# A four-block fp32 kernel on one Trainium2 core: cached keys taken transposed from a DRAM scratch, and the output projection of attention dealt out anew

## What is computed

```python
q = rope(rmsnorm(x @ Wq.T, q_norm_w)); k = rope(rmsnorm(x @ Wk.T, k_norm_w)); v = x @ Wv.T
kc = k_cache[block_table].reshape(bsz, 512, 8, 128)      # 16 pages of 32 keys per batch row
vc = v_cache[block_table].reshape(bsz, 512, 8, 128)
k_all, v_all = concat([kc, k], 1), concat([vc, v], 1)    # 640 keys
scores = einsum('bqhd,bkhd->bhqk', q, repeat(k_all, 4)) / sqrt(128)
scores = where(valid, scores, -1e30)                     # cached keys at or past cache_seqlens are masked
o = einsum('bhqk,bkhd->bqhd', softmax(scores), repeat(v_all, 4))
x = x + o.reshape(bsz, seqlen, 4096) @ Wo.T
```

## Time and profile before

| | |
|---|---|
| median of 3 runs | 1541.6 us |
| profiled execution | 1539.51 us, its span 1537.7 us |
| busy: PE, DVE, ACT, POOL | 96%, 73%, 55%, 49% of the span |
| mean granted TensorE clock | 0.987 |
| matmuls of PE | 8254 instructions |
| HBM read, written | 97.9 MB, 2.1 MB |

### The profile page before, as it was taken

The page is one execution under the profiler, slowest core; times in us unless marked ns, Lnnn a source line. Parts: engine busy times, 40 slices in busy tenths (PEclk is TensorE's granted clock), DMA queues, the critical chain, the costliest instruction groups (busy, mean ns, idle before and its releaser), DMA issues.

```text
span 1537.7 us, 27396 instructions
## 1 busy us (share of the span) xinstructions
PE 1468.6 (96%) x8254; PEld 1267.7 (82%) x8254; DVE 1117.8 (73%) x2224; ACT 851.5 (55%) x2024; POOL 750.0 (49%) x700
## 2 busy tenths in 40 slices
PE   3899999999999999999999999999997998999999
PEld 2788888888888888888888888888886776888887
DVE  4788888888888888888888888888885554122212
ACT  1566666666666666666666666666653233332331
POOL 5555565555655566555565555654440002433442
PEclk9899999999999999999999999999998999999999
DMA  4422222222222222222222222213202301331331
GB/s 123 136 62 77 59 59 65 63 67 72 59 64 65 62 75 60 63 65 71 67 59 64 64 65 74 59 46 110 52 15 59 87 0 39 108 102 51 104 102 63
DMA packets 107461, 105.99 MB, mean 69 GB/s; under 512 B 35873, under 2 KB 79393, under 8 KB 107073
## 3 DMA queue, kind: packets, MB, share of 16 engines
q1 hardware_dynamic: 107328, 104.42, 23.9%
HBM read 97.91 MB, written 2.10 MB: 65 GB/s over the span
## 4 chain that ended last, share of the span: by engine, by line
PE 72%; DVE 18%; issue 7%; ACT 1%; DMA 1%; POOL 1%; DVEq 0%; SPq 0%; ACTq 0%; POOLq 0%
PE banks L279 21%; PE banks L281 21%; PE banks L280 21%; PE banks L1106 8%; DVE pt_pair L739 3%; DVE k_sin L727 3%; DVE q_cos L720 3%; DVE kv_raw L733 2%; DVE w_pair L785 2%; DVE o_pair L739 1%; DVE k_cos L727 1%; DMA w_raw<-in_w_att 1%; PE banks L1171 1%; POOL w_pair L430 1%; DVE kv_raw L734 0%
## 5 line engine op out<-in xcount | busy, mean ns | idle before, releaser
L580 ACT ACTIVATE prob<-prob,nbias 128x640 f32<-128x640 f32 x256 | 210.2, 822 | 168.7 <-DVE nbias L763 168.7
L763 DVE CUSTOM_DVE_ANT_0 prob<-banks,mask,q_rs 128x640 f32<-128x640 f32 x256 | 219.5, 874 | 66.5 <-PE banks L281 66.4
L739 DVE TENSOR_TENSOR pt_pair<-banks,pt_pair 128x640 fp32r<-128x640 f32 x256 | 209.4, 818 | 61.2 <-ACT pt_pair L576 61.1
L576 ACT ACTIVATE pt_pair<-banks 128x640 fp32r<-128x640 f32 x256 | 179.2, 700 | 62.0 <-PE banks L1106 62.0
L1106 PE MATMUL banks<-ident,prob 128*128 128x128 f32 x1280 | 184.2, 275 | 19.1 <-DVE pt_pair L739 19.1
L773 DVE TENSOR_SCALAR prob<-prob,rsum 128x640 f32<-128x640 f32 x256 | 193.1, 754 | 9.1
L279 PE MATMUL banks<-w_pair,x_pair 128*128 128x256 f32 (+1 forms) x512 | 179.2, 350 | 21.1 <-POOL w_pair L430 21.1
L1106 PEld LDWEIGHTS banks<-ident,prob 128*128 128x128 f32 x1280 | 150.6, 141 | 49.7 <-issue 31.8
L509 POOL TENSOR_TENSOR fw_pair<-w_raw,fw_pair 128x1280 fp32r<-128x1280 f32 (+1 forms) x44 | 98.5, 2260 | 162.2 <-ACT fw_pair L672 154.6
L280 PE MATMUL banks<-w_pair,x_pair 128*128 128x256 f32 (+1 forms) x512 | 173.8, 339 | 0.0
L281 PE MATMUL banks<-w_pair,x_pair 128*128 128x256 f32 (+1 forms) x512 | 173.7, 339 | 0.0
(11 more groups left out here) (198 smaller groups left out, 3708.6 us busy)
## 6 DMA issues: line engine op xcount, KB each, us to landing
kv_raw<-in_kv SPq DMA_DIRECT2D x1024, 32.0 KB, 1.7
w_raw<-in_w_att SPq DMA_DIRECT2D x64, 320.0 KB, 3.0
w_raw<-in_fw SPq DMA_DIRECT2D x66, 256.0 KB, 2.9
x_raw<-in_xT SPq DMA_DIRECT2D x64, 256.0 KB, 3.1
w_raw<-gu_b SPq DMA_DIRECT2D x44, 64.0 KB, 2.9
acc<-in_x SPq DMA_DIRECT2D x1, 2048.0 KB, 10.5
w_raw<-in_w SPq DMA_DIRECT2D x2, 1024.0 KB, 5.3
out_x<-acc SPq DMA_DIRECT2D x8, 256.0 KB, 2.3
```

What stands on the lines that cost most here:

```text
L576: act.activation(pt_pair[:, 0, h].rearrange("p c n -> p (c n)"), pt_ps, ACT.Copy).then_inc(pt_hi, 1)
L580: act.activation(prob[:, h, :], prob[:, h, :], ACT.Exp, bias=nbias[:, h:h + 1], scale=-1.0, accum_out=psum_row[:, h:h + 1]).then_inc(exped, 1)
L739: dve.tensor_tensor(pair[1], src, pair[0].bitcast(F32), ALU.subtract).then_inc(lo_sem, 1)
L763: dve.tensor_tensor_reduce(out=prob[:, h, :].rearrange("p (a n) -> p a n", a=2), in0=score_ps[h % 2][:, :, 0:HALF], in1=mask[:, n % B, :]. ...
```

## The change

The host hands over a second copy of the key cache, `kT`, with each page transposed to heads x (128 x 32). A scratch tensor `kt_all` is made in DRAM, batch row x page slot x head x 128 x 32. In steps 0 to 7 SP, after the loads of the step, reads the page numbers of batch row n again and issues 16 DMAs from `kT` to `kt_all` (`gather_keys`), each 8 rows of 16 KB. From the second group on (steps 8 to 63) the cached keys of a step come with one DMA from `kt_all` to `kt_raw` (128 partitions, each 16 runs of 128 bytes), ahead of the step's page DMAs, which then carry only the values. ACT splits off the high half of `kt_raw` in a copy of its own (128x512) and that of the new keys from PSUM (128x128); POOL makes the cached keys' low half (`kc_low`), DVE that of the new keys alone. PE's cached-key transposes remain for steps 0 to 7 only. PE issues the 12 output matmuls as 2 ahead of the transposes of head 1, 8 after them and 2 after those of head 2. On DVE `w_high` stands ahead of `mask_min` of head 2, and `kt_low` ahead of `pt_low` of head 1. The scratch for dynamic DMA descriptors is 4096 instead of 8192.

```diff
--- before.py
+++ after.py
@@ -106,6 +106,7 @@
         x_pair = [sb(f"x_pair{i}", [P, 2, DC, P], F32R, where=att) for i in range(2)]
         kv_raw = sb("kv_raw", [P, 2, KC, 2 * D], where=att)
         v_pair = [sb(f"v_pair{i}", [P, 2, KC, D], F32R, where=att) for i in range(2)]
+        kt_raw = sb("kt_raw", [P, 2, CACHE], where=att)
         kt_pair = sb("kt_pair", [P, 2, KEYS], F32R, where=att)
         qt_pair = sb("qt_pair", [P, 2, REP, P], F32R, where=att)
         pt_pair = sb("pt_pair", [P, 2, REP, KC, P], F32R, where=att)
@@ -225,6 +226,9 @@
         k_rot = sem("k_rot")
         kt_done = sem("kt_done")
         kt_hi, kt_lo = sem("kt_hi"), sem("kt_lo")
+        s_gathered = [sem(f"s_gathered{b}") for b in range(B)]
+        s_ktin = [sem(f"s_ktin{i}") for i in range(2)]
+        kc_hi, kc_lo = sem("kc_hi"), sem("kc_lo")
         scored = sem("scored")
         masked = sem("masked")
         exped = sem("exped")
@@ -272,6 +276,8 @@
         td_done, td_own, td_hi, td_lo = sem("td_done"), sem("td_own"), sem("td_hi"), sem("td_lo")
         ffn_done, ffn_added = sem("ffn_done"), sem("ffn_added")
 
+        kt_all = nc.dram_tensor("kt_all", [B, NPP, HK, D, PSIZE], F32, kind="Internal").ap()
+
         block = ctx.enter_context(nc.Block())
 
         def product(e, dst, lhs, rhs, first, last):
@@ -302,18 +308,37 @@
             def load_w(m, par):
                 sp.dma_start(w_raw[:, par, :], t["w_att"][ds(m), :, :].rearrange("a p n -> p (a n)")).then_inc(s_win[par], 16)
 
-            def load_kv(n, par, used=False):
-                g, b = n // B, n % B
+            def load_pages(b):
                 _, pages = nc.values_load_multi_w_load_instructions(
                     t["pages"][ds(b), :], engines=[sp.engine], min_val=0, max_val=PAGES - 1,
                     skip_runtime_bounds_check_because="page numbers are below PAGES")
+                return pages
+
+            def load_kv(n, par, used=False):
+
+                g, b = n // B, n % B
+                pages = load_pages(b)
+                if g:
+                    if n >= B + 2:
+                        sp.wait_ge(kc_lo, n - B - 1)
+                    if g == 1:
+                        sp.wait_ge(s_gathered[b], 16 * NPP)
+                    sp.dma_start(kt_raw[:, par, :].rearrange("p (j s) -> p j s", s=PSIZE),
+                                 kt_all[b, :, g].rearrange("j d s -> d j s")).then_inc(s_ktin[par], 16)
                 if used:
                     sp.wait_ge(v_lo, n - 1)
                     sp.wait_ge(kt_done, n - 1)
+                at = D if g else 0
                 for j, page in enumerate(pages):
                     a = PSIZE * (j % 4)
-                    sp.dma_start(kv_raw[a:a + PSIZE, par, j // 4, :],
-                                 t["kv"][ds(g), ds(page), :, :].rearrange("g a s n -> s (g a n)")).then_inc(s_kvin[par], 16)
+                    sp.dma_start(kv_raw[a:a + PSIZE, par, j // 4, at:2 * D],
+                                 t["kv"][ds(g), ds(page), :, at:2 * D].rearrange("g a s n -> s (g a) n")).then_inc(s_kvin[par], 16)
+
+            def gather_keys(b):
+
+                for j, page in enumerate(load_pages(b)):
+                    sp.dma_start(kt_all[b, j].rearrange("g d s -> g (d s)"),
+                                 t["kT"][ds(page), :, :].rearrange("a g n -> (a g) n")).then_inc(s_gathered[b], 16)
 
             load_x(0, 0)
             load_w(0, 0)
@@ -356,6 +381,8 @@
             last_w = NT - PIECES - 1
             for n in range(NT - 2):
                 step(n, n % 2, x=n + 3 < NT, w=n < last_w)
+                if n < B:
+                    gather_keys(n)
                 if n == NT - PIECES + 1:
                     _, labels = nc.values_load_multi_w_load_instructions(
                         t["label"].unsqueeze(0), engines=[sp.engine], min_val=0, max_val=4,
@@ -435,6 +462,11 @@
                 pool.tensor_tensor(v_pair[par][:, 1], kv_raw[:, par, :, D:2 * D],
                                    v_pair[par][:, 0].bitcast(F32), ALU.subtract).then_inc(v_lo, 1)
 
+            def kc_low(n, par):
+                pool.wait_ge(kc_hi, n - B + 1)
+                pool.tensor_tensor(kt_pair[:, 1, 0:CACHE], kt_raw[:, par, :], kt_pair[:, 0, 0:CACHE].bitcast(F32),
+                                   ALU.subtract).then_inc(kc_lo, 1)
+
             def q_norm(n, par):
 
                 pool.wait_ge(q_sq, n + 1)
@@ -482,6 +514,8 @@
                     q_rotate(n + 1)
                     q_norm(n + 1, 1 - par)
                 v_low(n, par)
+                if nxt and n + 1 >= B:
+                    kc_low(n + 1, 1 - par)
                 if isinstance(n, int) and n == 0:
                     w_low(PIECES - 1, 1)
                 if x:
@@ -564,8 +598,12 @@
                 act.activation(qt_pair[:, 0].rearrange("p h n -> p (h n)"), q_ps, ACT.Copy).then_inc(qt_hi, 1)
 
             def kt_high(n):
+                new = slice(CACHE if n >= B else 0, KEYS)
                 act.wait_ge(kt_done, n + 1)
-                act.activation(kt_pair[:, 0], kt_ps, ACT.Copy).then_inc(kt_hi, 1)
+                if n >= B:
+                    act.wait_ge(s_ktin[n % 2], 16 * ((n - B) // 2 + 1))
+                    act.activation(kt_pair[:, 0, 0:CACHE], kt_raw[:, n % 2, :], ACT.Copy).then_inc(kc_hi, 1)
+                act.activation(kt_pair[:, 0, new], kt_ps[:, new], ACT.Copy).then_inc(kt_hi, 1)
 
             def o_high(n):
                 act.wait_ge(pv_done, n + 1)
@@ -742,7 +780,8 @@
                 low(qt_hi, n + 1, [qt_pair[:, k].rearrange("p h n -> p (h n)") for k in range(2)], q_ps, qt_lo)
 
             def kt_low(n):
-                low(kt_hi, n + 1, [kt_pair[:, k] for k in range(2)], kt_ps, kt_lo)
+                new = slice(CACHE if n >= B else 0, KEYS)
+                low(kt_hi, n + 1, [kt_pair[:, k, new] for k in range(2)], kt_ps[:, new], kt_lo)
 
             def o_low(n):
                 low(o_hi, n + 1, [o_pair[:, k].rearrange("p h n -> p (h n)") for k in range(2)], misc_ps, o_lo)
@@ -824,6 +863,10 @@
                 if not first:
                     pt_low(n - 1, 3)
                 normalise(n, 1)
+                if first:
+                    w_high(PIECES - 1, 1)
+                if w:
+                    w_high(n + PIECES, par)
                 mask_min(n, par, 2)
                 if nxt:
                     q_times_cos(n + 1)
@@ -831,19 +874,14 @@
                 normalise(n, 2)
                 if n + 1 < B:
                     make_mask(n + 1)
-                if first:
-                    w_high(PIECES - 1, 1)
-                if w:
-                    w_high(n + PIECES, par)
                 if not first:
                     o_low(n - 1)
                 pt_low(n, 0)
                 mask_min(n, par, 3)
                 if nxt:
                     qt_low(n + 1)
+                    kt_low(n + 1)
                 pt_low(n, 1)
-                if nxt:
-                    kt_low(n + 1)
                 normalise(n, 3)
                 pt_low(n, 2)
                 if not first:
@@ -1083,12 +1121,16 @@
 
             def transpose_new_k(n, par):
                 pe.wait_ge(k_rot, n + 1)
+                if n >= B:
+                    pe.wait_ge(masked, REP * (n - 1) + 3)
                 pe.transpose(kt_ps[:, CACHE:KEYS], kv_raw[:, par, KC - 1, 0:D], ident[:]).then_inc(kt_done, 1)
 
             def scores(n, h):
                 if h == 0:
                     pe.wait_ge(qt_lo, n + 1)
                     pe.wait_ge(kt_lo, n + 1)
+                    if n >= B:
+                        pe.wait_ge(kc_lo, n - B + 1)
                 elif h > 1:
                     pe.wait_ge(masked, REP * n + h - 1)
                 elif not (isinstance(n, int) and n == 0):
@@ -1118,15 +1160,17 @@
                                    c == 0, c == KC - 1)
                 last.then_inc(pv_done, 1)
 
-            def project_out(n, heads):
-                if heads[0] == 0:
+            def project_out(n, begin, end):
+
+                if begin == 0:
                     pe.wait_ge(o_lo, n + 1)
                     pe.wait_ge(w_lo, (n // B) * PIECES + PIECES)
                 at = group_at(n) + WWO
-                for h in heads:
-                    last = product(pe, misc_ps, lambda k: o_pair[:, k, h, :],
-                                   lambda k: w_pair[:, k, ds(at + h * HID, HID)], h == 0, h == REP - 1)
-                if heads[-1] == REP - 1:
+                for i in range(begin, end):
+                    h, (j, k) = i // 3, ((0, 0), (0, 1), (1, 0))[i % 3]
+                    last = pe.matmul(misc_ps, o_pair[:, j, h, :], w_pair[:, k, ds(at + h * HID, HID)],
+                                     start=i == 0, stop=i == 3 * REP - 1)
+                if end == 3 * REP:
                     last.then_inc(wo_done, 1)
 
             def step(n, par, x=True, w=True, nxt=True):
@@ -1145,14 +1189,17 @@
                 scores(n, 3)
                 if nxt:
                     transpose_q(n + 1)
```

(14 more changed lines are left out.)

## The result

The changed kernel takes 1572.9 us (median of 4 runs), the kernel before on the same chip 1541.6 (median of 4, 1537.0 to 1541.8). The ratio is 1.0211, 95% interval 1.0195 to 1.0227. The loss is clear of the 3 us that the prediction gives as visible, while the interval lies on both sides of 2%; the direction is the one forecast (1564, range 1530 to 1590). The profiled execution took 1573.1 us, its span 1571.3, against 1539.5 and 1537.7.

The account below looks back on a forecast made before the run. PE's own work and a VectorE chain were taken to set the step, SP's issue queue the first group. On 1541.6 us, +50.0 (queue) + 4 (rings) + 2 (clock) - 32.9 (steady steps) gave +23, said as 1564, range 1530 to 1590.

Parts of the forecast that it names:

- What bounds: Attention step of 17.48 us: set by PE's own work and a VectorE chain freeing `pt_ps`, with a 0.37 us PE pause.
- The steady step: Attention steps after the first group: gain of 0.62 us a step, between 0.2 and 0.87.
- The pause of 0.19: PE before the third transposes of the probabilities: a new wait of 0.19 us, behind ScalarE's two copies and VectorE's low half.
- The gathers on the issue queue: SP in steps 0 to 7: cycle 24.7 us against a step of 17.88, loss 50.0 us by step 9.
- The lag on the rings: DMA rings after gather issue: eight rows on eight engines hold up the last weight piece once, 4 us.
- The clock: PE behind step 9: waiting may drop the clock to 1.2 GHz, 2 us once, bounds 0 and 7.
- The key load: Steps 8 to 63: one 256 KB DMA in 128-byte runs, landing in 3 to 4 us, hidden, costing zero.
- The sum: Whole kernel: +50.0 + 4 + 2 less 32.9 for 53 steps, +23 us, said as 1564.
- (a): SP in steps 0 to 7 isn't the bound: 1535 if the reading is cheap (0.10), 1505 without any stall (0.12).
- (b): Eight DMA rings bound the gathers in steps 0 to 7: 1645 at 2 us a row, 1583 at 1.5; chance 0.11.
- (c): Steady steps lose their gain to pauses: 0.2 us a step, 11 us instead of 33, 1586; chance 0.10.
- (d): Strided key load is slow from step 8 on: at 25 us a step already 1990; chance 0.02.

Follow-up runs that it names:

- the keys alone: Changed kernel with keys by DMA from fixed pages, no gathers or second reading, output projection 9 and 3, old VectorE order: 1536.8 us, 0.9995 of the kernel before.
- the order alone: Changed kernel with all keys still transposed on PE and nothing gathered, keeping the new output projection and VectorE order: 1521.5 us, 0.9904 of the kernel before.

## Why the prediction was right, point by point

- **What bounds.** Right: the wait ended by VectorE and PE's own work together set the step. With the keys alone the time stayed the same, with the order alone PE was without a pause.
- **The steady step.** Forecast 0.62 a step, measured 0.69 (17.49 to 16.80). The next scores came 4.56 us behind the query's transposes; the working gave 4.65. The term that was too large is ScalarE's second copy: from 637.17 to the next piece are 0.16 us, not 0.22, and the first 0.52. The pause of 0.19 left over shrank to 0.08 (16.80 against 17.16 - 0.44). I had overlooked a piece of evidence in the kernel before. Its last six steps have no `w_high`, and its timeline shows the pause closed there, with the steps at 17.17:

```profile
1050.96 0.27 PE L1086 MATMUL banks<-ident,kv_raw 128*128 128x128 f32 x1
1051.12 0.74 PE L1106 MATMUL banks<-ident,prob 128*128 128x128 f32 x5
```

- It also corrects a count: those six steps had 0.37 to gain, not 0.69. 47 x 0.69 + 6 x 0.37 = 34.7, less 2.6 for step 10, which lasted 19.4; measured 32.6.
- **The gathers on the issue queue.** The mechanism was right, with its place, its slope and its end: PE late from step 2 on, weights late in steps 8 and 9. The size of one term was off: 0.52 us for a gather's issue; it was 0.67 to 0.73 (11.75 for sixteen at 69.74), 8.35 of the sum become 10.7 to 11.8. That is 22.3 us more over eight steps. The second reading was about 3.0 instead of 3.6 (4.9 less in eight), a new key load 0.65 on the queue instead of 1.4 (1.5 less in two), and the queue started 1.0 later. The last weights were issued at 272.8, not 253.3. Behind that the sum hits 280.3 (272.8 + 3.0 + 4.5) only because two errors cancel: VectorE had the weights 4.0 us after their issue (276.80), and the query's transposes followed 3.5 later (280.33). The prediction gave the issue bounds of 0.35 and 0.8 us but did not carry them into its own range: 16 x 0.28 x 8 = 36 us more at 0.8, so 1600.
- **The lag on the rings, +4.** Wrong in size. A gather landed in 2.6 us and a weight piece behind the gathers in 3.8 instead of 3.0, so the lag is under 1 us. In the stretch of sixteen gathers, 152 to 163.3 us, the DMA view of the kernel after reads (packets in all and by size; then packets, MB, share of 16 engines):

```profile
DMA packets 456, 1.90 MB, mean 168 GB/s; under 512 B 224, under 2 KB 224, under 8 KB 224
...
q1 hardware_dynamic: 456, 1.90, 61.4%
```

- 61.4% of 16 is 9.8 engines busy on average, so more than eight. The 232 larger packets carry 1.90 MB, 8 KB each, half a row. The page DMA: Bandwidth & Descriptors of the Trainium skill ("Why a DMA increments its semaphore by 16 and not by 1") takes the slowest dimension as the instruction carries it; the prediction read eight off the kernel's text. Measured, this gather isn't moved as eight rows. Its rows lie one behind the other on both sides, and the packets fit one run of 128 KB cut in 16, an inference; the instruction itself isn't on record.
- **The clock, +2.** Right. Step 10 lasted 19.4 instead of 16.8, 2.6 over. PE stood idle for 10.2 us ahead of 280.33, and the windows behind show the granted clock at half, the lower level of 1.2 GHz, and then full:

```profile
280.00:282.00 2.00, 1.52 (x6) 1.13 (x7) 1.97 (x6) 0.64 (x3) 1.83 (x3) 0.50 0.22 45
...
286.00:288.00 2.00, 2.00 (x14) 1.78 (x13) 0.48 (x2) 0.87 (x2) 1.76 (x2) 1.00 0.21 43
```

- From 282 to 284 it is 0.50 too, from 284 to 286 0.65. Some 5 us at half speed lose 2.5, an estimate, which is the 2.6. In 60 to 300 us the granted clock was 0.86.
- **The key load, 0.** Right: its landing was 3.0 us, and the kernel without gathers has it in full. The factor of 19 that the page VectorE: DVE Perf Modes of the Trainium skill gives ("The three transpose paths") is for a copy that transposes by its strides, with a large innermost stride at the destination, measured against the transposing DMA; the 3.0 us show that it has no hold on this load of whole runs.
- **The sum.** +50 + 4 + 2 - 33 = +23 was forecast; +69.7 - 32.6 - 3.5 = +33.6 was measured. Of the 10.6 between them the longer first group is 19.7, and the clock 0.6. Against these stand the lag of 4 that never came, 2.3 more of steady gain (the 32.6 hold step 10's loss of 2.6, so 35.2 for 32.9) and the 3.5 behind the attention: 19.7 + 0.6 - 4 - 2.3 - 3.5 = 10.5. So the time came within 9 us of the forecast in part by luck; the loss alone was forecast 28% too small, 50.0 for 69.7.
- **The rivals.** (a) falls: the kernel without the second reading shows the queue's slope as worked out. (b), (c) and (d) fall by the landing times, the step of 16.80 and the kernel without gathers.

## What to carry to other kernels

Add up the issue queue's cycle, register loads and all, for each stage by itself, before work is moved to it: under the step's length more of it is free, above it each microsecond costs in every step. Spread one-time work until the cycle is just below the step; here that, with the page numbers read once instead of twice, turned +31 us into -35. Where a step waits for a bank, edits on both sides of the wait are worth their sum only together, so try them together as well as one by one.

## What the runs showed of the hardware

- A DMA of about 128 KB from DRAM to DRAM took SP 492 ns to issue, written as 8 rows that touch, as 16, or as 16 that don't, against 316 for a page load of 32 rows to SBUF; as eight rows that don't touch 627, though it moved a quarter of the bytes.
- A load of 2048 runs of 128 bytes took 378 ns to issue and 3.0 us to land, no more than the 256 KB of x in long rows (3.2).
- Four transposes of 128x128 on PE took 1.12 us at a granted clock of 0.50 (from 280.33) and 0.60 at 1.00 (from 618.74).
